# Gate of an attention + mixture-of-experts kernel: fewer split products, packed bias rows, logits turned back by transposes

## The reference, cut to what matters

```python
x = layernorm(x + attention(x, W_qkv, W_o))      # x: 16 x 1024 x 256, 16 heads of 16, causal, rotary
gate = softmax(x @ Wg + bg)                      # 8 experts
topk_vals, topk_idx = top_k(gate, 2)             # the two best experts of each token
gate_sparse = einsum('bsk,bske->bse', topk_vals, one_hot(topk_idx, 8))
gate_sparse = gate_sparse / sum(gate_sparse, axis=-1, keepdims=True)
y = einsum('bsi,eoi->bseo', x, We) + be          # every expert, with its bias row be[e]
out = einsum('bseo,bse->bso', y, gate_sparse)
x = layernorm(x + out)
```

## Time and profile before

| | |
|---|---|
| median of three runs | 3325.67 us |
| the profiled execution | 3333.02 us, its span 3331.3 us |
| TensorE busy | 3209.5 us (96%) |
| VectorE busy | 2690.4 us (81%) |
| ScalarE busy | 1888.8 us (57%) |
| GpSimd busy | 1212.4 us (36%) |
| mean granted clock of TensorE | 0.969 of 2.4 GHz |

### The profile page before, as it was taken

How to read it: one execution, slowest core, us unless ns; L and a number is a source line. 1 busy time by engine, 2 the same in 40 slices (tenths; PEclk the granted TensorE clock), 3 DMA queues, 4 the chain that set the end, 5 groups by cost and what they waited for, 6 DMA issues and landing times. The chain is left out here.

```text
span 3331.3 us, 59099 instructions
## 1 busy us (share of the span) xinstructions
PE 3209.5 (96%) x19072; PEld 1791.1 (54%) x19072; DVE 2690.4 (81%) x8349; ACT 1888.8 (57%) x4257; POOL 1212.4 (36%) x1418
## 2 busy tenths in 40 slices
PE   5789999999999999999999999999999999999987
PEld 2234555555555555555555555555555555555555
DVE  5777878888888888878888888888888888888734
ACT  2266556565655656556565655656565565655540
POOL 4153424343242443424344342434334243431110
PEclk8699999999999999999999999999999999999987
DMA  6344324333432434344233433333343243334000
GB/s 139 57 68 74 63 56 73 62 66 64 80 59 53 75 56 73 58 78 63 50 76 57 83 58 70 66 56 69 62 80 63 55 71 65 67 64 63 2 26 13
DMA packets 174789, 210.97 MB, mean 63 GB/s; under 512 B 25992, under 2 KB 124560, under 8 KB 174224
## 3 DMA queue, kind: packets, MB, share of 16 engines
q1 hardware_dynamic: 173056, 202.98, 34.9%
q10 hardware_dynamic: 1424, 4.21, 0.3%
HBM read 138.43 MB, written 67.11 MB: 62 GB/s over the span
## 5 line engine op out<-in xcount | busy, mean ns | idle before, releaser
L642 ACT ACTIVATE weights<-scores 128x512 f32<-128x512 f32 (+3 forms) x3072 | 1336.3, 494 | 959.8 <-PE scores L963 950.7
L760 DVE CUSTOM_DVE_ANT_0 bank<-bank,far_q 128x128 f32<-128x128 f32 (+3 forms) x2048 | 962.6, 513 | 222.0 <-PE bank L947 208.1
L947 PE MATMUL bank<-k_stack,q_stack 96*128 96x512 bf16 (+3 forms) x3072 | 811.8, 336 | 36.8 <-DVE maxima L763 9.6
L963 PE MATMUL scores<-q_stack,k_stack 99*128 99x512 bf16 (+3 forms) x3072 | 825.3, 330 | 11.0 <-ACT weights L642 7.3
L559 POOL TENSOR_SCALAR_AFFINE_SELECT weights<-weights 128x512 f32<-128x512 f32 x512 | 326.3, 638 | 1296.4 <-ACT weights L642 1296.3
L763 DVE TENSOR_REDUCE maxima<-bank 128x1 f32<-128x512 f32 x1024 | 645.0, 682 | 75.8 <-PE bank L947 73.4
L985 PE MATMUL attend<-weights,values 128*32 128x512 f32 (+3 forms) x6144 | 582.3, 494 | 1.0 <-POOL weights L559 0.9
L963 PEld LDWEIGHTS scores<-q_stack,k_stack 99*128 99x128 bf16 x3072 | 280.8, 98 | 419.0 <-ACT weights L642 155.3
L947 PEld LDWEIGHTS bank<-k_stack,q_stack 96*128 96x128 bf16 x3072 | 278.9, 99 | 413.8 <-issue 162.4
L890 PE MATMUL bank<-wexp_hi,zT_hi 128*128 128x512 f32 x1024 | 389.4, 462 | 0.1
L864 DVE SCALAR_TENSOR_TENSOR z<-bank,gates,z 128x256 f32<-128x256 f32 x512 | 247.2, 483 | 142.3 <-PE bank L890 135.3
(11 more groups left out here) (105 smaller groups left out, 3299.7 us busy)
## 6 DMA issues: line engine op xcount, KB each, us to landing
parts_scratch<-parts SPq DMA_DIRECT2D x128, 384.0 KB, 2.5
q_stack<-parts_scratch SPq DMA_DIRECT2D x384, 128.0 KB, 7.2
k_stack<-parts_scratch SPq DMA_DIRECT2D x384, 128.0 KB, 7.8
x_in<-in_x SPq DMA_DIRECT2D x64, 256.0 KB, 2.9
z<-in_x SPq DMA_DIRECT2D x32, 512.0 KB, 4.6
out<-z SPq DMA_DIRECT2D x32, 512.0 KB, 2.9
q_stack<-maxrow SPq DMA_DIRECT2D x192, 8.0 KB, 2.6
z<-in_w_exp ACTq DMA_DIRECT2D x1, 1024.0 KB, 14.3
```

The source lines that it names most:

```text
L642: act.activation(weights[:, n % NW, hh, c0:CH], st[(QUAD * n + hh) % NS][:, c0:CH], ACT.Exp, scale=DH ** -0.5).then_inc(S["weights_ready"], 1)
L760: dve.tensor_tensor_reduce(out=b[:, 0:w], in0=b[:, 0:w], in1=far_q[:, CH - w:CH], scale=1.0, scalar=-SENTINEL, op0=ALU.add, op1=ALU.max, a ...
L947: pe.matmul(b[:, 0:w], q_stack[0:ROWS, n, hh, qt * P:(qt + 1) * P], k_stack[0:ROWS, n, hh, kc * CH:kc * CH + w], start=True, stop=True).th ...
L963: pe.matmul(st[(QUAD * n + hh) % NS][:, c0:CH], k_stack[0:MROWS, s, hh, kb * P:(kb + 1) * P], q_stack[0:MROWS, s, hh, qc * CH + c0:(qc + 1 ...
```

## The change

The gate's stationary operand holds both parts of the weights side by side (columns 0 to 7 the rounded part, 8 to 15 the rest), so `GL` issues four products instead of six (against `zT_hi` and `zT_lo`), and makes 16 rows. ScalarE adds the bias to 16 rows (zero for the second eight). `GLT` uses four `transpose` instructions of 16 rows, and VectorE adds the two parts of each logit with a `tensor_reduce` over PSUM. For the bias rows, `GB` writes three copies of the gates to `gates_parts` (rounded, rest, full), `GT` transposes 24 columns, and `BE` multiplies 24 rows of float32r gates with 24 rows (rounded bias twice, rest once) in one float32r product where a float32 one stood. `gates` becomes an alias of `picked`. At the start the bias rows are loaded three times and split by VectorE, in front of its list; the gate's bias transfer comes last. The rows change their places in SBUF (`logitsT` at partition 32 of a new `lowrows`, which also holds `maxrow`).

```diff
-W_LOADS = 7
+W_LOADS = 9
-    "YT": 1, "WO": 2, "N2": 1, "MT": 2, "GA": 3, "GB": 4, "MOE": 1,
+    "YT": 1, "WO": 2, "N2": 1, "MT": 2, "GA": 3, "GB": 6, "MOE": 1,
...
-                    act.activation(gatesT[:, :], b[0:NE, :], ACT.Copy).then_inc(fr, 1)
+                    act.activation(gatesT[:, :], b[0:NR, :], ACT.Copy).then_inc(fr, 1)
...
-                             (bexp[:, :], b_exp),
-                             (bgate[0:NE, :], b_gate.rearrange("(n o) -> n o", o=1))):
+                             *((bias_raw[NE * i:NE * (i + 1), :], b_exp) for i in range(3))):
                 act.dma_start(dst, src).then_inc(S["w_loaded"], DMA)
+            act.wait_ge(S["bias_zeroed"], 1)
+            act.dma_start(bgate[0:NE, :], b_gate.rearrange("(n o) -> n o", o=1)).then_inc(S["w_loaded"], DMA)
...
+            dve.wait_ge(S["w_loaded"], W_LOADS * DMA)
+            dve.tensor_copy(bias_hi, bias_raw).then_inc(S["bias_split"], 1)
+            dve.wait_ge(S["bias_split"], 1)
+            dve.tensor_tensor(bexp, bias_raw, bias_hi.bitcast(F32), ALU.subtract).then_inc(S["bias_split"], 1)
+            dve.wait_ge(S["bias_split"], 2)
+            dve.tensor_copy(bexp[0:2 * NE], bias_hi[0:2 * NE]).then_inc(S["bias_split"], 1)
+            dve.wait_ge(S["bias_split"], 3)
...
-                    dve.tensor_copy(logits[:, :, 0:NE], b[:, 0:4 * NE].rearrange("p (t e) -> p t e", t=4)).then_inc(fr, 1)
+                    dve.tensor_reduce(logits[:, :, 0:NE], b[:, 0:8 * NE].rearrange("p (t i e) -> p t e i", t=4, i=2), AX.X,
+                                      ALU.add).then_inc(fr, 1)
...
-                    dve.tensor_tensor(gates[:, :, :], picked[:, :, :],
-                                      gate_sum[:, 1].unsqueeze(2).to_broadcast([P, 4, NE]), ALU.mult) \
-                        .then_inc(S["gates_ready"], 1)
+                    link(c, step, dve.tensor_tensor(gates[:, :, :], picked[:, :, :],
+                                      gate_sum[:, 1].unsqueeze(2).to_broadcast([P, 4, NE]), ALU.mult))
+                    link(c, step, dve.tensor_copy(gates_parts[:, :, 0:NE], gates[:, :, :]))
+                    dve.tensor_copy(gates_parts[:, :, 2 * NE:], gates[:, :, :])
+                    dve.tensor_tensor(gates_parts[:, :, NE:2 * NE], gates[:, :, :], gates_parts[:, :, 0:NE].bitcast(F32),
+                                      ALU.subtract).then_inc(S["gates_ready"], 1)
...
-                    split_matmul(b[:, :], lambda i, kt: (wgate_hi, wgate_lo)[i][:, kt],
-                                 lambda j, kt: (zT_hi, zT_lo)[j][:, kt]).then_inc(fu, 1)
+                    for i, zT in enumerate((zT_hi, zT_lo)):
+                        for kt in range(KT):
+                            last = pe.matmul(b[:, :], wgate_parts[:, kt], zT[:, kt], start=i + kt == 0, stop=i + kt == KT)
+                    last.then_inc(fu, 1)
...
-                        last = pe.matmul(b[:, t * NE:(t + 1) * NE], logitsT[:, t * P:(t + 1) * P], ident[0:NE, 0:NE],
-                                         start=True, stop=True)
+                        last = pe.transpose(b[:, 2 * NE * t:2 * NE * (t + 1)], logitsT[:, t * P:(t + 1) * P],
+                                            ident[32:32 + 2 * NE, 32:32 + 2 * NE])
...
-                        last = pe.transpose(b[0:NE, t * P:(t + 1) * P], gates[:, t], ident[:, :])
+                        last = pe.transpose(b[0:NR, t * P:(t + 1) * P], gates_parts[:, t].bitcast(F32), ident[:, :])
...
-                        last = pe.matmul(b[:, tt * D:(tt + 1) * D], gatesT[:, t * P:(t + 1) * P], bexp[:, :],
+                        last = pe.matmul(b[:, tt * D:(tt + 1) * D], gatesT[:, t * P:(t + 1) * P], bexp,
                                          start=True, stop=True)
```

More of the change, by code:

```diff
@@ L21 @@
 NE = 8
+NR = 3 * NE
 TILES = T // P
@@ L75, in diagonal @@
     return kb * P >= qc * CH
-PE_WORK = {"XT": 2, "QK": 8, "VP": 8, "ST": 1, "PV": 4, "YT": 2, "HT": 2, "WO": 8, "ZT": 2, "GL": 6, "GLT": 1,
+PE_WORK = {"XT": 2, "QK": 8, "VP": 8, "ST": 1, "PV": 4, "YT": 2, "HT": 2, "WO": 8, "ZT": 2, "GL": 4, "GLT": 1,
            "GT": 2, "BE": 4, "MOE": 6, "MT": 1}
@@ L346, in attention_moe_kernel @@
         wgate = sb("wgate_sb", [P, KT, NE])
-        wgate_hi = sb("wgate_hi", [P, KT, P], F32R)
-        wgate_lo = sb("wgate_lo", [P, KT, P], F32R)
+        wgate_parts = sb("wgate_parts", [P, KT, P], F32R)
         bgate = sb("bgate_sb", [P, 1])
@@ L383, in attention_moe_kernel @@
         zT_lo = sb("zT_lo", [P, KT, CH], F32R)
-        narrow = sb("narrow", [P, CH + D])
-        logitsT = narrow[0:NE, 0:CH]
-        gatesT, bexp = narrow[32:32 + NE, 0:CH], narrow[32:32 + NE, CH:CH + D]
+        lowrows = sb("lowrows", [P, CH])
+        maxrow_err = lowrows[0:QUAD * TILES, 0:P]
+        maxrow = lowrows[0:QUAD * TILES, P:P + 3 * P // 2].bitcast(BF16).rearrange("p (a q) -> p a q", a=3)
+        narrow = sb("narrow", [P, CH + D], F32R)
+        logitsT = lowrows[32:32 + 2 * NE, :]
+        gatesT, bexp = narrow[32:32 + NR, 0:CH], narrow[32:32 + NR, CH:CH + D]
+        bias_raw, bias_hi = head_out[64:64 + NR, 0:D], narrow[64:64 + NR, 0:D]
         logits = sb("logits", [P, 4, 2 * NE])
@@ L394, in attention_moe_kernel @@
         gate_sum = sb("gate_sum", [P, 2, 4])
-        gates = sb("gates", [P, 4, NE])
+        gates = picked
+        gates_parts = sb("gates_parts", [P, 4, NR], F32R)
         st = [ctx.enter_context(nc.psum_tensor(f"scores{i}", [P, CH], F32)) for i in range(NS)]
@@ L401, in attention_moe_kernel @@
         names = [*COUNTED, "link", "rest_ready", "parts_ready", "turning", "sp_waits", "pool_waits", "dve_waits",
-                 "zeroed", "zeroed_v", "const_v", "const_p", "ident_ready", "w_loaded", "we_loaded", "hi_split", "w_split"]
+                 "zeroed", "zeroed_v", "bias_zeroed", "bias_split", "const_v", "const_p", "ident_ready", "w_loaded", "we_loaded", "hi_split", "w_split"]
         names += [f"{n}{i}" for n in ("stack", "maxrow") for i in range(SLOTS)]
@@ L680, in work @@
                     filled(act, c, step)
-                    act.activation(logitsT[:, :], b[0:NE, :], ACT.Identity, bias=bgate[0:NE, :]).then_inc(fr, 1)
+                    act.activation(logitsT[:, :], b[0:2 * NE, :], ACT.Identity, bias=bgate[0:2 * NE, :]).then_inc(fr, 1)
                 elif kind == "GA":
@@ L717, in hold @@
                 dve.sem_inc(S["dve_waits"], 1)
-            dve.memset(wgate_hi[:, :, :].bitcast(F32), 0.0).then_inc(S["zeroed_v"], 1)
-            dve.memset(wgate_lo[:, :, :].bitcast(F32), 0.0).then_inc(S["zeroed_v"], 1)
+            dve.memset(bgate[:, :], 0.0).then_inc(S["bias_zeroed"], 1)
+            dve.memset(wgate_parts[:, :, :].bitcast(F32), 0.0).then_inc(S["zeroed_v"], 1)
             dve.memset(logits[:, :, NE:], SENTINEL).then_inc(S["const_v"], 1)
@@ L726, in _ @@
             dve.wait_ge(S["ident_ready"], 1)
-            dve.wait_ge(S["zeroed_v"], 2)
+            dve.wait_ge(S["zeroed_v"], 1)
             dve.wait_ge(S["const_v"], CONST_V)
+            dve.wait_ge(S["w_loaded"], W_LOADS * DMA)
[5 more added lines that the diff above has]
+            dve.wait_ge(S["bias_split"], 3)
             def split_weights():
@@ L736, in split_weights @@
                     dve.tensor_copy(wexp_hi[:, kt], w).then_inc(S["hi_split"], 1)
-                    dve.tensor_copy(wgate_hi[:, kt, 0:NE], wgate[:, kt]).then_inc(S["hi_split"], 1)
+                    dve.tensor_copy(wgate_parts[:, kt, 0:NE], wgate[:, kt]).then_inc(S["hi_split"], 1)
                 dve.wait_ge(S["hi_split"], 2 * KT)
@@ L741, in split_weights @@
                     dve.tensor_tensor(wexp_lo[:, kt], w, wexp_hi[:, kt].bitcast(F32), ALU.subtract)
-                    last = dve.tensor_tensor(wgate_lo[:, kt, 0:NE], wgate[:, kt], wgate_hi[:, kt, 0:NE].bitcast(F32),
-                                             ALU.subtract)
+                    last = dve.tensor_tensor(wgate_parts[:, kt, NE:2 * NE], wgate[:, kt],
+                                             wgate_parts[:, kt, 0:NE].bitcast(F32), ALU.subtract)
                 last.then_inc(S["w_split"], 1)
```

2 lines of the change are left out of this document (removed).

## The result

| | before | after |
|---|---|---|
| median of the runs | 3325.71 us (n = 5) | 3256.74 us (n = 5) |
| lowest and highest | 3320.12, 3330.49 us | 3254.24, 3258.12 us |
| ratio, 95% interval | 1 | 0.9784 [0.9773, 0.9795] |
| span of the profiled execution | 3331.3 us | 3255.0 us |

A forecast was written before the change was run, and what follows sets the result against it. The prediction took TensorE to set the pace in most places and VectorE in some. Its terms, 6 + 25.5 + 21.5 + 7.5 - 1.3, were summed to 60 us off 3325.7, giving 3266 us, range 3230 to 3298.

The forecast's parts named there:

- clock, 15 turns: In the turns of `mid`, the falls of the clock behind `BE` go as it gets shorter: 21.5 us gained.
- less work, 15 turns: In the turns of `mid`, 0.4 us gained on each half 0 and 1.7 on each half 1.
- `post`: In the last two halves, at the lower clock, shorter steps less the longer chain: 3.75 us per half, 7.5 gained.
- start: At the start, two more transfers on ScalarE and the bias split on VectorE: 1.3 us lost.
- `GL`, `GLT`, `BE` on TensorE: TensorE's list in each half gets shorter by 0.49, 0.54 and 1.27 us, 2.30 together.
- what VectorE's longer chain takes back: In `GB` and `GLT`, gates come 0.6 us later per half; only 0.25 and 0.45 of 1.03 us saved get through.
- Half 0 absorbs `BE`, half 1 pays it: Behind `BE`, its 1.27 us saving gives only 0.18 us on half 0 but all of it on half 1.
- `GT` will wait for the gates: In front of `GT`, TensorE gets a new wait, shown by an idle entry of about 0.5 us in each half.
- The full saving: Rival: VectorE follows everywhere and all 2.30 us per half arrive; 98 us gained, 3228 us; chance 0.13.
- Staying falls: Rival: the falls of the clock stay, at the same place or elsewhere; 38 us gained, 3287 us; chance 0.14.
- The slower kernel: Rival: GpSimd holds up the three new operations of `GB`, gates come 4.2 us later; 3375 us; chance 0.05.

The follow-up runs named there:

- e3: The kernel before, with the four float32 matmuls of `BE` contracting all 128 rows, `narrow` zeroed at the start; 3298.23 us, ratio 0.9912.
- e12: e9 with only the first 8 rows contracted, leaving out the two bias correction terms; 3310.99 us, ratio 0.9947 against the kernel before.
- e9: The kernel after, with each product of `BE` issued four times on both halves, 24 rows; 3282.12 us, ratio 0.9859 against the kernel before.
- e2: The kernel after, with six products in `GL` and float32 matmuls in `GLT`, so the bias part alone; 3291.60 us, ratio 0.9893 against before.
- e1: The kernel before with the new `GL` and `GLT` only; gates, `GT` and `BE` as they were; 3282.13 us, ratio 0.9866.
- e6: The kernel after, with two more linked copies of the gates on VectorE in `GB`; 3277.79 us, ratio 0.9851 against the kernel before.
- e7: The kernel after, with `GT` moved behind the next scores in the list; 3260.26 us, ratio 0.9793 against the kernel before.
- e10: The kernel after, with one multiplication writing two copies of the gates, one linked step fewer; 3252.92 us, ratio 0.9773 against the kernel before.
- e4: The kernel after, with twelve extra products of 128 rows ahead of `BE`'s own on half 0; 3278.06 us, ratio 0.9848 against the kernel before.
- e8: The kernel after, with `MT` of half 0 moved behind `BE` in the list; 3246.55 us, ratio 0.9757 against the kernel before.

## Why the prediction was right, and where it was off

| term, us | predicted | measured |
|---|---|---|
| clock, 15 turns | 21.5 | 25 to 27 in the profiled executions, 17 to 20 by the medians |
| less work, 15 turns | 31.5 | 42 to 44 |
| `post` | 7.5 | 7.3 |
| start | -1.3 | -0.1 |
| all | 59 (written as 60) | 76.3 by the spans, 69.0 by the medians |

Two errors offset each other in part: the work saved was put 11 to 13 us too low, and the clock, on the scale of the medians, 1 to 4 too high. So the 9 us between forecast and result are less than the mis-sized term.

- **The clock** is right in size. Before to e3 is 30.1 by the medians, less 6.1 in `post` (82.5 to 76.4) and 3.6 of shorter steps: 20; the other count gives 24.7 less 7.3, 17. The 7.3 is what the profiled execution of before lay above its median, and I took a price read from that execution off the median as it was. Its runs tell that falls make up such differences: of eleven on one chip the fastest (3315.3 us) had a mean clock of 0.975, the slowest (3335.3) of 0.967. The reason that I gave was wrong, or at least not the one that decides. I wrote that the falls would go because `BE` becomes a third as long, and I costed 24 rows instead of 8 at nothing. For the product's own time that is nearly so (e3). But the rows are what keeps the clock up: e3 keeps nearly the length and loses the falls, e12 has float32r products and keeps them, e9 has a `BE` of 2.10 us on 24 rows and one fall. That this term came out is in part luck: what I priced at nothing is what lets the falls go. The kernel after has both, fewer microseconds and more rows; how a short `BE` on 8 rows would do was not tried.
- **`GL`, `GLT`, `BE` on TensorE**: 0.49, 0.54, 1.27 predicted; 0.46, 0.64, 1.21 measured, together 2.31 for 2.30.
- **The mis-sized term is what VectorE's longer chain takes back.** I took 0.6 us per half in full, and let only 0.25 and 0.45 us of the 1.03 through. By itself the chain did grow so (e2: 0.53 and 0.52), but it takes back less than 1.2 us of a turn: e2's turn is 0.72 shorter where `BE` alone would give 1.2, so 0.5; from e1 to after it is 0.92, so 0.3. The saving of `GL` and `GLT` came through with 2.04 us in a turn (e1). In the kernel after the chain grew only from 5.37 to 5.78 and from 5.09 to 5.15, since an earlier list leaves less idle time in it and other operations are held up by GpSimd: on half 1 e1 has 4.30 with the old chain, 0.42 less because the multiplication that writes the gates is not held there, and some 0.3 less idle; in the kernel after L864 is held by 0.32. So the turn fell by 195.29 - 192.33 = 2.96 us instead of 2.1.
- **Half 0 absorbs `BE`, half 1 pays it**: right, by e9.
- **`GT` will wait for the gates**: right, though by 0.27 us under the record before it, not by the idle entry of 0.5 that I named as its sign. e6 shows the wait in every half, e7 that moving `GT` only hands it to `BE`; what e10's shorter chain gets back is hardly clear of the noise.
- **`post`**: right as a sum, but the terms in it don't stand as I added them. e3, with `GLT` and `BE` as before, already has 6.1 of the 7.3, at a mean clock of 0.88 instead of 0.79. After, the instructions are short (`BE` 1.12 us by starts instead of 3.68, 2.56 saved for 2.5 predicted), but the clock there is 0.82, so which part of the 7.3 is whose isn't settled:

```profile
3175.58 0.61 PE L1049 MATMUL bank<-ident,lowrows 16*128 16x16 f32 x4 [0.77 <-ACT lowrows L684]
3179.79 1.03 PE L1057 MATMUL bank<-ident,gates_parts 128*24 128x128 f32 x4 [3.60 <-DVE gates_parts L866]
3181.58 1.19 PE L1065 MATMUL bank<-narrow 24*128 24x256 f32 x4 [0.77 <-ACT narrow L693]
```

- **The rule of the Trainium skill** (VectorE: DVE Perf Modes, The DRAIN you can't avoid), that the semaphore costs nothing extra, does not hold for operations as small as these: in the kernel after they start 0.22 us apart with a link, 0.09 without. (The 21 us of e6 are no measure of it, since e6 adds whole copies with their links.)
- **The rivals.** The full saving (69 + 21.5 + 7.4) lay too low, since half 0 absorbs `BE` and the chain takes some. Staying falls are excluded by the clock of 1.00. The slower kernel had its mechanism right, GpSimd holding up the new operations, and its size wrong: L864 takes 0.50 us on half 1, where GpSimd is at work in one of 0.69 (611.62 to 612.31), and L849 had 0.61 there before; on half 0 L857 takes 0.65 in most turns, and its predecessor L844 had 0.59. None is held by microseconds.
- The two parts overlap: alone they bring 46 us (e1) and 37 (e2), together 69, since either one removes some or all of the falls.

## What to carry to other kernels

Where one engine is busy for 99% of the time, read the timelines of two engines side by side: a saving is worth nothing where the other engine sets the stretch, and all of itself where that engine has a gap; here the same added products cost 0 on one half and 1.3 us on the other (e9). A chain that becomes what the critical engine waits for must be counted in links, and its price read in place, since waits inside it shrink too. A VectorE operation that is slow in one place only should be looked up in GpSimd's timeline: two steps later it may meet a shorter operation, which here gave 10 us. If the clock of TensorE falls behind some step, try that step on more rows before making it shorter: nearly the same time on 128 rows gave 30 us.

## What the hardware showed that was not expected

- Two microseconds of TensorE work on 8 rows are followed by a fall to the 1.2 GHz level in 18 of 30 halves (float32, before) or 20 of 30 (float32r, e12); on 24 rows in one (e9), on 128 rows in none (e3). The cost is 25 to 29 us of the run. With the same `BE` as before, e1 has only 10, so rows aren't all of it.
- float32r products of 256 columns follow each other by 0.12 us on the same rows, 24 (e9) or 128 (e4); where operands of 128 and of 24 rows follow each other, the step is 0.21 or 0.31 (e4). Float32 ones are recorded as two MATMULs with steps of 0.216 us on 8 rows (before) and on 128 (e3).
- A VectorE operation on 32 partitions x 128 with its operands in SBUF takes 0.28 us, 0.61 or 1.37; the long ones start while GpSimd is at work and end about 0.14 us behind its operation (after, e8).
- The same copy of 128 x 32 takes 0.18 us, or 0.50 where it starts within a GpSimd operation, whose end it follows by 0.04 us (e6).
